# Last feed-forward: layers two and three in four 64x64 tiles of TensorE, and the second relu taken together with the gates by VectorE

## The reference

```
# E, D, H, TOP_K = 6, 64, 64, 2
rh = relu(features @ router_w1 + router_b1)
expert_logits = softmax(rh @ router_w2 + router_b2)
top_w, top_i = top_k(expert_logits, 2)
routing_weights = softmax(top_w)
h1 = relu(einsum('bsd,edh->bseh', features, expert_w1) + expert_b1)
h2 = relu(einsum('bseh,ehf->bsef', h1, expert_w2) + expert_b2)
expert_out = einsum('bsef,efo->bseo', h2, expert_w3) + expert_b3
sel = take_along_axis(expert_out, top_i[:, :, :, None], axis=2)
combined = sum(sel * routing_weights[..., None], axis=2)
...
h = h + combined
```

## Time and profile before

| | before |
|---|---|
| median of 3 runs | 1331.05 us (1328.56 to 1332.08) |
| the profiled execution, its own time | 1327.24 us |
| its span in the profile | 1325.4 us |
| mean granted TensorE clock | 0.917 |
| PE busy | 1216.7 us (92%) |
| PEld busy | 788.5 us (59%) |
| DVE busy | 780.4 us (59%) |
| ACT busy | 639.8 us (48%) |
| POOL busy | 521.0 us (39%) |

### The profile page before, as it was taken

One profiled execution on the slowest core, in us unless ns is written; L12 is line 12 of the kernel. 1 busy time (PEld: TensorE's weight loads), 2 busy tenths in 40 slices (PEclk: granted clock), 3 DMA queues, 4 the chain that ended last, 5 costly groups with the idle time before them and its releaser, 6 DMA issues.

```text
span 1325.4 us, 27084 instructions
## 1 busy us (share of the span) xinstructions
PE 1216.7 (92%) x10227; PEld 788.5 (59%) x10227; DVE 780.4 (59%) x1724; ACT 639.8 (48%) x1369; POOL 521.0 (39%) x1109
## 2 busy tenths in 40 slices
PE   7999999999999999999999996899618888888997
PEld 6665666666666666666666664545316675775553
DVE  4565655655566566566665652143678998985442
ACT  2336555555554555555555542150254664734564
POOL 2112445744644555546445553308861030421100
PEclk9989999999999999999999998899757668568999
DMA  4100000000000000000000001111110000000000
GB/s 85 18 4 2 2 2 2 5 5 2 4 2 2 2 2 2 2 2 2 2 2 3 2 2 33 64 64 20 17 12 1 1 1 1 13 1 0 13 14 22
DMA packets 33983, 14.55 MB, mean 11 GB/s; under 512 B 30644, under 2 KB 31252, under 8 KB 33855
## 3 DMA queue, kind: packets, MB, share of 16 engines
q1 hardware_dynamic: 29247, 10.92, 3.7%
q0 software_dynamic: 4608, 1.91, 1.6%
HBM read 6.43 MB, written 7.27 MB: 10 GB/s over the span
## 4 chain that ended last, share of the span: by engine, by line
PE 72%; DVE 11%; issue 5%; POOL 5%; ACT 4%; DMA 1%; SPq 0%; POOLq 0%; DVEq 0%; ACTq 0%
PE psum L761 21%; PE psum L742 10%; PE psum L667 9%; PE psum L733 8%; PE psum L717 4%; POOL XN L1321 3%; PE psum L1016 2%; PE psum L652 2%; DVE arena L2015 2%; PE psum L996 1%; PE psum L573 1%; PE psum L560 1%; PE psum L817 1%; PE psum L830 1%; PE psum L1031 1%
## 5 line engine op out<-in xcount | busy, mean ns | idle before, releaser
L1443 ACT ACTIVATE arena<-psum 125x500 f32<-125x500 f32 x576 | 306.8, 585 | 329.6 <-PE psum L742 329.6
L1816 DVE TENSOR_REDUCE arena<-psum 125x1 f32<-125x500 f32 x384 | 242.6, 674 | 184.3 <-PE psum L667 184.3
L667 PE MATMUL psum<-arena 32*125 32x500 f32 (+1 forms) x1536 | 321.9, 515 | 0.3 <-DVE arena L1803 0.3
L761 PE MATMUL psum<-arena,XN 125*64 125x250 f32 x2304 | 307.1, 387 | 0.2 <-ACT arena L1443 0.2
L742 PE MATMUL psum<-arena 32*125 32x250 f32 x2304 | 289.9, 368 | 0.0
L742 PEld LDWEIGHTS psum<-arena 32*125 32x125 f32 x2304 | 213.5, 182 | 11.2 <-issue 0.5
L761 PEld LDWEIGHTS psum<-arena,XN 125*64 125x64 f32 x2304 | 140.0, 136 | 120.8 <-issue 78.0
L1819 DVE TENSOR_REDUCE arena<-psum 125x2 f32<-125x500 f32 x192 | 121.4, 674 | 69.1 <-PE psum L667 64.9
L667 PEld LDWEIGHTS psum<-arena 32*125 32x125 f32 x1536 | 127.3, 182 | 3.3 <-ACT arena L1434 0.8
L733 PE MATMUL psum<-arena,onesb 3*125 3x500 bf16 x576 | 122.2, 421 | 0.0
L1213 POOL TENSOR_TENSOR lnst<-lnst,mhalf 125x12 f32<-125x12 f32 x12 | 27.4, 2286 | 204.5 <-DVE lnst L1771 204.4
(11 more groups left out here) (351 smaller groups left out, 1943.7 us busy)
## 6 DMA issues: line engine op xcount, KB each, us to landing
arena<-arena SPq DMA_DIRECT2D x192, 1.5 KB
expert_in<-XN SPq DMA_DIRECT2D x8, 256.0 KB, 4.8
arena<-expert_in SPq DMA_DIRECT2D x4, 512.0 KB, 5.2
expert_out<-arena SPq DMA_DIRECT2D x4, 512.0 KB, 2.6
out<-H SPq DMA_DIRECT2D x16, 93.8 KB
expert_in<-XN,slot_in POOLq DMA_INDIRECT x48
XN<-expert_out,slot_out POOLq DMA_INDIRECT x48, 3.8
arena<-in_L_ffn_w SPq DMA_DIRECT2D x2, 256.0 KB
```

The costliest lines, as they stand in the source:

```text
L667: last = pe.matmul(ps[0:R, at_:at_ + hi - lo], QH[row:row + 32, b, g, j * R:(j + 1) * R], KH[row:row + 32, b, g, lo:hi], start=True, stop= ...
L761: last = pe.matmul(ctx_bank[64 * h2:64 * h2 + 64, 0:THIRD], XN[:, p, c, a, :], PR[:, x % 4, h2, i * THIRD:(i + 1) * THIRD], start=(c == 0) ...
L1443: act.activation(PR[:, x % 4, h2, :], st_bank[(2 * x + h2) % 3][0:R, 0:2 * THIRD], ACT.Exp)\
L1816: dve.reduce_max(MX[:, q % 2, 0, 2 * h2 + tile:2 * h2 + tile + 1], ps[0:R, 0:2 * THIRD], AX)\
```

## The change

`layer2` becomes four matmuls of 64x64: row tile `e` holds the second weights of expert `e` of the pair, once for each column tile. Row tile `e` reads the 64 rows of `H1` that belong to expert `e`, of both sequences, and writes to a bank of its own, which then holds one expert and, on its two halves, the two sequences (in crossed order for the second expert). `e2w` has no zeros any more. `layer3` likewise becomes twelve 64x64 matmuls and two for the bias, and since two row tiles write to two banks, its result is in two parts: ScalarE copies the first to `YS` and VectorE adds the second (a new `summed` on VectorE).

ScalarE no longer takes the second relu. It copies the gates out of PSUM (`gates_out`), and VectorE's `gated` reads layer two from PSUM: relu(y + b) is written as max(y, -b) + b, so VectorE takes max(y, -b) times the gate in one instruction, and the missing b times the gate goes through the third layer into its bias. That third bias, `b3r`, gets the product of `expert_b2` and the third weights added once, by six small matmuls (`bias3`) and one VectorE add after `logit` of the first pair. GpSimd lays out `BB` for it and negates `e2b`.

```diff
@@ TensorE
-                                            GP[:, p % 2, 2 * j:2 * j + 2].rearrange("r a c -> r (a c)"),
+                                            GP[:, p % 2, j].rearrange("r s c -> r (s c)"),
+            def bias3():
+                pe.wait_ge(S["b2_laid"], 1)
+                ps, done = take(pe, ("b3",))
+                for n in range(6):
+                    last = pe.matmul(ps[:, 0:D], BB[:, 128 * n:128 * n + 128], e3w[0:64, n // 2, n % 2, :],
+                                     start=(n == 0), stop=(n == 5))
+                last.then_inc(done, 1)
...
                 for a in range(2):
                     emptied(pe, ("l1", k, a))
-                    ps, done = take(pe, ("l2", k, a))
-                    pe.matmul(ps[:, 0:HALF], e2w[:, ep, :], H1[(2 * k + a) % 4], start=True, stop=True)\
-                        .then_inc(done, 1)
+                out2 = [take(pe, ("l2", k, e)) for e in range(2)]
+                for c in range(2):
+                    for e in range(2):
+                        r = slice(64 * e, 64 * e + 64)
+                        ps, done = out2[e]
+                        last = pe.matmul(ps[64 * c:64 * c + 64, 0:HALF], e2w[r, ep, :],
+                                         H1[(2 * k + (c + e) % 2) % 4][r], start=True, stop=True,
+                                         tile_position=(64 * e, 64 * c))
+                        if c:
+                            last.then_inc(done, 1)
...
                 for ep in range(3):
-                    for a in range(2):
-                        emptied(pe, ("gate", 3 * n + ep, a))
-                ps, done = take(pe, ("l3", n))
-                for a in range(2):
-                    pe.matmul(ps[64 * a:64 * a + 64, 0:HALF], b3r[:, a, :], GT[:, p % 2, th * HALF:(th + 1) * HALF],
-                              start=True, stop=False, tile_position=(0, 64 * a))
+                    for e in range(2):
+                        emptied(pe, ("l2", 3 * n + ep, e))
+                out3 = [take(pe, ("l3", n, e)) for e in range(2)]
+                for e in range(2):
+                    r = slice(64 * e, 64 * e + 64)
+                    pe.matmul(out3[e][0][r, 0:HALF], b3r[r], GT[r, p % 2, th * HALF:(th + 1) * HALF],
+                              start=True, stop=False, tile_position=(64 * e, 64 * e))
                 for ep in range(3):
-                    for a in range(2):
-                        last = pe.matmul(ps[64 * a:64 * a + 64, 0:HALF], e3w[:, ep, :], H2[6 * (n % 2) + 2 * ep + a],
-                                         start=False, stop=(ep == 2), tile_position=(0, 64 * a))
-                last.then_inc(done, 1)
+                    for c in range(2):
+                        for e in range(2):
+                            r, o = slice(64 * e, 64 * e + 64), (c + e) % 2
+                            ps, done = out3[e]
+                            last = pe.matmul(ps[64 * o:64 * o + 64, 0:HALF], e3w[r, ep, c, :],
+                                             H2[6 * (n % 2) + 2 * ep + c][r], start=(ep == 0 and c == 1),
+                                             stop=(ep == 2), tile_position=(64 * e, 64 * o))
+                            if ep == 2 and c:
+                                last.then_inc(done, 1)
...
                 elif kind == "logit":
                     logit(x)
+                    if not x:
+                        bias3()
@@ GpSimd, event "room"
-                    pool.memset(b3r, 0.0)
-                    pool.memset(e2w, 0.0).then_inc(S["late_zero"], 1)
+                    pool.memset(b3r, 0.0).then_inc(S["late_zero"], 1)
...
+                    link(pool.memset(BB, 0.0))
...
+                    for e in range(2):
+                        pool.tensor_copy(spots[:, e, :, 0], bias2[:, e])
+                        link(pool.tensor_copy(spots[:, e, :, 70], bias2[:, e]))
+                    pool.tensor_scalar(W["e2b"], W["e2b"], -1.0, None, ALU.mult).then_inc(S["b2_laid"], 1)
@@ ScalarE
-            def hidden2(k):
-
-                ep = steps1[k][2]
+            def gates_out(k):
+
                 for a in range(2):
-                    ps, done = filled(act, ("l2", k, a))
+                    ps, done = filled(act, ("gate", k, a))
                     if k >= 2:
-                        emptied(act, ("gate", k - 2, a))
-                    act.activation(H2R[(2 * k + a) % 4], ps[:, 0:HALF], ACT.Relu, bias=W["e2b"][:, ep:ep + 1])\
-                       .then_inc(done, 1)
+                        emptied(act, ("l2", k - 2, a))
+                    act.activation(GS[(2 * k + a) % 4], ps[:, 0:HALF], ACT.Copy).then_inc(done, 1)
@@ VectorE
-                dve.tensor_copy(GP[:, p % 2, :, 0:E1], GW)\
+                dve.tensor_copy(GP[:, p % 2, :, :, 0:2 * E1],
+                                GW.rearrange("r (j a) e -> r j (a e)", a=2).unsqueeze(2)
+                                .to_broadcast([R, NJ, 2, 2 * E1]))\
...
-                    emptied(dve, ("l2", k, a))
-                    g, done = filled(dve, ("gate", k, a))
+                    emptied(dve, ("gate", k, a))
+                    h, done = filled(dve, ("l2", k, a))
...
-                    dve.tensor_tensor(H2[6 * (n % 2) + 2 * ep + a], H2R[(2 * k + a) % 4], g[:, 0:HALF], ALU.mult)\
-                       .then_inc(done, 1)
+                    floor = W["e2b"][:, 2 * ep + a:2 * ep + a + 1]
+                    dve.scalar_tensor_tensor(H2[6 * (n % 2) + 2 * ep + a], h[:, 0:HALF], floor, GS[(2 * k + a) % 4],
+                                             ALU.max, ALU.mult).then_inc(done, 1)
+
+            def summed(n):
+
+                emptied(dve, ("l3", n, 0))
+                ps, done = filled(dve, ("l3", n, 1))
+                dve.tensor_tensor(YS[:, n % 2, :], YS[:, n % 2, :], ps[:, 0:HALF], ALU.add).then_inc(done, 1)
...
                 elif kind == "step":
                     if 1 <= x <= len(steps1):
                         gated(x - 1)
+                    if x >= 4 and x % 3 == 1:
+                        summed(x // 3 - 1)
```

More of the change, by code:

```diff
@@ L223, in build @@
         GT, _ = view(CV1 + NJ * 256, [2, L])
-        H2R = [arena[:, TC1 + 2 * NJ * 128 + n * HALF:TC1 + 2 * NJ * 128 + n * HALF + HALF] for n in range(4)]
+        GS = [arena[:, TC1 + 2 * NJ * 128 + n * HALF:TC1 + 2 * NJ * 128 + n * HALF + HALF] for n in range(4)]
         e1w, at = view(0, [3, 128])
-        e2w, at = view(at, [3, 128])
-        e3w, at = view(at, [3, D])
+        e2w, at = view(at, [3, D])
+        e3w, at = view(at, [3, 2, D])
         SEL, at = view(at, [3, 2, D])
-        ramp, at = view(at, [6])
-        b3r, at = view(at, [2, D])
-        GP, at = view(at, [2, 2 * NJ, D], parts=R)
+        ramp, at = view(at, [3, 2])
+        b3r, at = view(at, [D])
+        GP, at = view(at, [2, NJ, 2, D], parts=R)
         RH, at = view(at, [2, L])
@@ L240, in build @@
         assert at <= 4 * 2 * L, at
+        BB, at_b = view(at - 2 * HALF, [6 * 129], parts=64)
+        assert at_b <= 4 * 2 * L, at_b
         S = {}
@@ L1002, in gate_spread @@
                 emptied(pe, ("gt", p, th))
-                for a in range(2):
-                    r = slice(64 * a, 64 * a + 64)
-                    ps, done = take(pe, ("gate", k, a))
-                    pe.matmul(ps[:, 0:HALF], SEL[r, ep].rearrange("r e d -> r (e d)"),
+                for e in range(2):
+                    r = slice(64 * e, 64 * e + 64)
+                    ps, done = take(pe, ("gate", k, e))
+                    pe.matmul(ps[:, 0:HALF], SEL[r, ep].rearrange("r a d -> r (a d)"),
                               GT[r, p % 2, th * HALF:(th + 1) * HALF], start=True, stop=True,
-                              tile_position=(64 * a, 0)).then_inc(done, 1)
+                              tile_position=(64 * e, 0)).then_inc(done, 1)
             def layer2(k):
@@ L1019, in layer3 @@
             def layer3(n):
                 p, th = divmod(n, 2)
+                if not n:
+                    emptied(pe, ("b3",))
                 for ep in range(3):
-                    for a in range(2):
-                        emptied(pe, ("gate", 3 * n + ep, a))
-                ps, done = take(pe, ("l3", n))
-                for a in range(2):
-                    pe.matmul(ps[64 * a:64 * a + 64, 0:HALF], b3r[:, a, :], GT[:, p % 2, th * HALF:(th + 1) * HALF],
-                              start=True, stop=False, tile_position=(0, 64 * a))
@@ L1035, in turned @@
             def turned(n):
-                emptied(pe, ("l3", n))
+                emptied(pe, ("l3", n, 1))
                 ps, done = take(pe, ("yt", n))
@@ L1613, in gate_tiles @@
                     if p >= 2:
-                        k = jobs[("l3", 2 * (p - 2) + 1)]
+                        k = jobs[("l3", 2 * (p - 2) + 1, 1)]
                         act.wait_ge(full[k % 8], k // 8 + 1)
@@ L1629, in summed @@
             def summed(n):
-                ps, done = filled(act, ("l3", n))
+                ps, done = filled(act, ("l3", n, 0))
```

(6 more changed lines are left out.)

32 lines of the change are left out of this document (20 added, 12 removed).

## The result

| | before | after |
|---|---|---|
| median of 10 runs each, us | 1328.67 (1323.09 to 1332.9) | 1311.93 (1310.23 to 1319.72) |
| profiled execution, us | 1327.24 | 1315.56 |
| its span, us | 1325.4 | 1313.4 |

The ratio of the times is 0.9889, with a 95% interval of 0.9871 to 0.9908: 14.8 us less (12.2 to 17.1). The forecast was 9.35 us less, so the direction was right and the time fell outside the range.

The account below looks back on a forecast made before the run. TensorE bounds most of the last chain, VectorE's routing the stretches before gates. Eight stretch terms sum to -10.35 us, the clock's +1.0 makes -9.35: 1317.9 profiled, 1321.7 as median (3.8 above); range 1317.5 to 1326.5.

Parts of the forecast that it names:

- Term 1: Up to the first gates: bias3's wait for a PSUM bank delays TensorE about 1 us, partly hidden by idle; +0.5 us.
- term 3: From the second gates to the third logits, on TensorE: three layer twos, 0.68 us less each; -2.3 us.
- Terms 2, 4, 7 and 8: Second gates 0; third gates' chain +0.55; last TensorE stretch, ten layer twos, -6.8; tail, VectorE's add after ScalarE's copy, +0.55 us.
- Terms 5 and 6: From third to fourth gates: four layer twos on TensorE, -2.7 us; then TensorE waits for VectorE's chain, only -0.15 us.
- Two at a time: Rival, chance 0.07: only two of four tiles run at once; layer two gains nothing, layer three slows; about 1345 us.
- The clock's term: TensorE's clock falls in longer idle ahead of second and third gates: +1.0 us (between 0 and 3.2), 1.7 behind the third.

Follow-up runs that it names:

- e2: The kernel before with only bias3's work added (six matmuls and a VectorE add into a spare place): 1323.39 us, ratio 0.9964 to before.
- e4: The changed kernel with layer two as two whole 128x128 matmuls again, using layer one's weights (another output): 1324.35 us, ratio 0.9974 to before.
- e5: The changed kernel with the gates' transposes placed later, two events for the second and third pair, one for the fourth: 1314.09 us, ratio 0.9900 to before.
- e6: The kernel before with four transposes of the identity on TensorE ahead of its wait for the first gates: 1323.43 us, ratio 0.9970 to before.
- e7: The changed kernel with 24 and 18 transposes of the identity ahead of the waits for the second and third gates: 1319.08 us, ratio 0.9929 to before.
- e8: The changed kernel run once more with nothing altered, beside e5 to e7 on the same chip: 1313.32 us, ratio 0.9900 to before.
- e10: e5 with the steps placed ahead of the layer norm and router in every engine's list, in the last stretch: 1316.14 us, ratio 0.9909 to before.
- e1: The changed kernel without bias3 and its VectorE add, leaving out the second bias's share of the output: 1318.31 us, ratio 0.9938 to before.
- e3: The changed kernel without bias3 and without the moved relu (ScalarE keeps it, VectorE multiplies by the gates): 1322.36 us, ratio 0.9975 to before.
- e9: The changed kernel with 16 transposes of the identity filling TensorE's wait for bias3's bank: 1318.12 us, ratio 0.9932 to before.

## Where the prediction was right, and where it was wrong

The stretch from the first gates to the second logits puts the runs in a row:

| idle ahead of the first gates, us | kernels | stretch, us |
|---|---|---|
| none | after, e2, e4, e5, e6, e7, e8, e10 | 10.35 to 11.29 |
| 0.65 to 0.69 | before, e1, e3 | 14.55 to 15.56 |
| 2.33 | e9 | 13.12 |

**Term 1 failed**, "I take +0.5; bounds: 0, if it hides, and 1.5, if nothing hides", with the part on the clock, which starts where "TensorE was granted 1.00 (2.4 GHz) from 1200 us on". The delay was rightly seen and costs 0.2 us. But the bounds excluded a gain. The prediction saw that the 0.65 us of idle would be filled, and read it as cover for the delay only. It had the mean clock of 0.63 in 1170 to 1180, and asked only where the clock would fall, not what kept it down up to 1200. For the last 9 us or so the gap did: 4.8 us between the profiles of before and after, 4.8 by the ratio when `bias3`'s work is added to before (e2), 4.0 when the gap alone is filled (e6). With it the sum is -9.35 - 0.5 + 0.2 - 4.8 = -14.45, and measured were -14.8 (12.2 to 17.1 less). That they meet so closely is partly luck: from the masked products to the end, the two traces of the changed kernel are 12.8 and 13.2 us shorter than that of before, because term 3 and the clock, below, gave less than forecast. The Trainium skill's "TensorE: Matmul & The Clock Gate", Part 1, has throttled as the state that the clock starts from, and activity as what releases it. Read so, idle time while the clock is still down can put off its rise; the table agrees for 0.65 us.

**Terms 2, 4, 7 and 8** hold within 0.1 us. Terms 5 and 6, -2.85 together, are -2.55 in e7 and -2.64 in e9, where the clock doesn't fall on the way (25.17 and 25.08 us for before's 27.72). **Term 3** was -1.6 rather than -2.3. The prediction counted the changes of tile shape within a step alone; what follows a layer two meets one too that it didn't meet before. The chain has, before and after,

```profile
1236.25 1.31 PE psum L950 x12
...
1230.77 1.51 PE psum L952 x12
```

for the router's matmuls behind a layer two, 0.2 us more. Another 0.3 to 0.4 is layer three, which with a wait took 2.88 us there (1220.02 to 1222.90) rather than 2.52, and the rest lies ahead of it.

**The layers.** 0.68 less a step was forecast and 0.67 measured. In these two layers row and column tiles compose with no loss beyond the change of shape. Two at a time, which had a chance of 0.07, is excluded by L1031's 0.79 us.

**The clock's term** was +1.0, with 1.7 for a fall behind the third gates. That fall came, at 1245, and its price is shown by two runs without it. From the third gates to the fourth, after needs 26.71 us and e8 26.65. With the clock at 1.00 throughout, e7 needs 25.17 and e9 25.08. So it cost 1.5 to 1.6 us. The 3.4 us of work that the prediction put at half speed came from none of its rows; after's 0.57 from 1245 to 1249 agrees with it. The fall behind the second gates was there too. In e8 it lasted about twice as long as in after:

```profile
1207.00:1215.00 8.00, 7.17 (x29) 3.80 (x30) 4.85 (x11) 3.65 (x10) 3.74 (x2) 0.57 0.00 0
```

and the stretch from the second gates to the third logits is the same 20.8 us in both, so a longer fall cost nothing there, as forecast.

**The moved relu** was credited with 0.3 us and is worth about 4.6 (e3 against e1). The prediction took it as settled that a step would take TensorE's 2.24 us, from counts of busy time (4.4 and 6.9 us under 9.7). With the relu on ScalarE and the gates' multiplication waiting for it, the counts would be as harmless, and yet TensorE waits. The terms of the last ten steps came out right since the kernel has the whole change; the argument for them was thin. VectorE's combined instruction takes 604 ns and not 545; the forecast of the last stretch holds all the same.

**The start** was high: 3.8 us were added for the median of three runs above the profiled execution, where ten have 1.4. The profiled execution of after, in turn, is 3.6 above its median. Of the 9.8 us between forecast and median, 5.4 are the change itself, by the ratio, 2.4 are this start, and 2.0 are what the difference of the two medians (16.7) has above the ratio's 14.8.

## What to carry to other kernels

Before pricing a delay on an engine, look at the granted clock on both sides of the idle time that it fills: at half clock a gap well under 1 us, closed by a few useless matmuls, was worth 4 us, and a filler placed where it made another gap gained nothing. Here, small tiles that use the array in both directions could be priced from rows of each direction alone, with the change of shape added; count the changes of shape in what follows the tiles too. A sum of busy times under the step's time doesn't show that a double-buffered chain keeps up; follow which bank is freed last.

## What the runs showed of the hardware that was not expected

- The clock's fall after a gap isn't set by the gap alone: 3.16 us ahead of the third gates brought 0.57 from 1245 to 1249 in after, and the same 3.16 us in e9 none, with 25.08 us to the fourth gates. The Trainium skill says in "TensorE: Matmul & The Clock Gate", Part 1, that the window of the activity monitor is free-running and doesn't reset when a kernel starts; that fits, and no run here separates it from other causes.
- A copy on VectorE took 1.50 to 1.54 us beside a GpSimd instruction of 1.47, and 0.20 where GpSimd was idle. An instruction of the router on VectorE (L2104) took 1.22 us beside the same GpSimd line ahead of the first gates of after, and 0.23 ahead of the third. In before and e9 the copy is what sets the first gates; in after it ends 0.1 us before they start, and TensorE comes there at that moment too. That GpSimd's work is the cause is argued from their coinciding, not tested.
- Executions differ by 5 us through the clock of a stretch far from the change, where the kernels are alike (the 12 us near 80 us at 1.00 in after and at 0.54 in e7). Marks within the program repeated to about 0.4 us over the first stretch and to 0.1 over the rest where the spans differed by 3.6.
